# First attention of a two-layer kernel: probabilities normalised in the 16-bit cast, one PSUM bank for each head's queries

## The reference, cut to what matters

```
q, k, v = einsum('bsx,xAnh->Abnsh', input, qkv * c1)      # 16 heads of 64
q = q + q_bias
a = einsum('bnqh,bnkh->bnqk', q, k) * 64 ** -0.5
a = a + relative_causal(einsum('bnqh,nvh->bnqv', q, emb) * 64 ** -0.5)
a = softmax(where(tril, a, -1e9))                          # 512 x 512, causal
o = einsum('bnqk,bnkh->bqnh', a, v).reshape(b, s, 1024)
out = o @ (out_kernel * c2) + out_bias
x = layernorm(x + out)
```

## Time and profile before

| | |
|---|---|
| median of 3 runs | 1677.52 us (1674.55 to 1745.03) |
| the profiled execution | 1676.82 us |
| its span in the profile | 1675.1 us |
| granted TensorE clock, mean | 0.948 of 2.4 GHz |
| busiest engines over the span | PE 85%, DVE 75%, ACT 58%, POOL 53% |

### The profile page before, as it was taken

How to read it: one execution, slowest core, us unless ns; L and a number is a source line. 1 busy time by engine, 2 the same in 40 slices (tenths; PEclk the granted TensorE clock), 3 DMA queues, 4 the chain that set the end, 5 groups by cost and what they waited for, 6 DMA issues and landing times. The chain is left out here.

```text
span 1675.1 us, 38178 instructions
## 1 busy us (share of the span) xinstructions
PE 1421.9 (85%) x12519; PEld 834.2 (50%) x12519; DVE 1262.4 (75%) x2722; ACT 971.0 (58%) x1921; POOL 879.9 (53%) x1203
## 2 busy tenths in 40 slices
PE   4899989898998999897589887489899899898736
PEld 3566666666666666665356555123333333332216
DVE  3788888887888888886688888377787787777534
ACT  2677767676776767675244443156666666665431
POOL 2877778777787777775445555211221221222524
PEclk9899999999999999999699999599999999999977
DMA  5645545454454545544000000411011011010001
GB/s 160 123 113 127 123 98 125 97 122 110 110 125 105 114 111 118 116 110 94 0 2 0 0 0 0 146 48 35 27 39 36 26 39 36 26 40 28 13 12 27
DMA packets 372881, 116.47 MB, mean 70 GB/s; under 512 B 341675, under 2 KB 369312, under 8 KB 372704
## 3 DMA queue, kind: packets, MB, share of 16 engines
q1 hardware_dynamic: 369472, 111.36, 27.9%
q10 hardware_dynamic: 1824, 3.15, 0.6%
q0 software_dynamic: 1536, 1.34, 0.3%
HBM read 20.36 MB, written 12.89 MB: 20 GB/s over the span
## 5 line engine op out<-in xcount | busy, mean ns | idle before, releaser
L541 ACT ACTIVATE prob<-score_ps,nmax 128x512 f32<-128x512 f32 (+3 forms) x512 | 264.9, 526 | 209.0 <-DVE nmax L594 209.0
L1563 DVE TENSOR_REDUCE a_nm<-a_s 128x1 f16<-128x512 f32 x512 | 324.8, 687 | 55.5 <-PE a_s L1335 53.6
L1489 ACT ACTIVATE a_pt<-a_st 128x1024 f32<-128x1024 f32 x256 | 260.4, 1021 | 131.4 <-PE a_st L1353 116.3
L130 POOL TENSOR_TENSOR gate<-mhalf 128x1 f32<-128x1 f32 (+1 forms) x284 | 124.2, 437 | 259.3 <-ACT k L566 137.6
L1335 PE MATMUL a_s<-a_kop,a_qop 128*128 128x512 f16 x512 | 199.6, 391 | 64.2 <-DVE a_nm L1563 47.4
L606 DVE SCALAR_TENSOR_TENSOR p<-prob,p 128x1280 f16<-128x1280 f32 x128 | 204.6, 1598 | 49.8 <-ACT p L550 49.8
L594 DVE TENSOR_REDUCE nmax<-score_ps 128x1 f32<-128x512 f32 (+3 forms) x512 | 213.0, 475 | 3.4 <-PE score_ps L455 3.3
L452 PE MATMUL score_ps<-k_h,q_h 128*128 128x512 f16 (+3 forms) x512 | 158.2, 309 | 22.4 <-ACT prob L541 14.2
L550 ACT ACTIVATE p<-prob 128x1280 f16<-128x1280 f32 x128 | 163.8, 1279 | 6.5
L888 ACT ACTIVATE hid<-fps,b_cols 128x512 f32<-128x512 f32 x130 | 86.3, 687 | 127.2 <-PE fps L848 127.2
L694 POOL TENSOR_TENSOR q_l<-q,q_h 128x512 f16<-128x512 f32 x130 | 152.9, 1176 | 10.8
(11 more groups left out here) (331 smaller groups left out, 3433.5 us busy)
## 6 DMA issues: line engine op xcount, KB each, us to landing
a_qop<-q_parts SPq DMA_DIRECT2D x32, 128.0 KB
a_kop<-k_parts SPq DMA_DIRECT2D x128, 24.0 KB
x_tok<-in_L_attn_input_dram SPq DMA_DIRECT2D x4, 512.0 KB, 12.3
pt<-p SPq DMA_TRANSPOSE x128, 4.1
e_w<-in_L_ffn_w_dram SPq DMA_DIRECT2D x1, 2048.0 KB, 8.3
q_parts<-a_q_h SPq DMA_DIRECT2D x16, 128.0 KB
k_parts<-a_k_h SPq DMA_DIRECT2D x16, 128.0 KB
out_dram<-a_res SPq DMA_DIRECT2D x8, 256.0 KB
```

Of the source, the lines that this page charges most:

```text
L541: ins = nc.scalar.activation(prob[h][:, P_OFF[c]:P_OFF[c] + w], score_ps[u][:, col:col + w], ACT.Exp, bias=nmax[h][:, c:c + 1], accum_out= ...
L1489: nc.scalar.activation(pt[kc % 2][r][:, :, :], st_ps[r][:, :, :], ACT.Exp, scale=1.0 / SC).then_inc(exp_done[r], 1)
L1563: nc.vector.tensor_reduce(nm[g % 2][:, c, hh:hh + 1], s_ps[c % 2][:, :], AX.X, ALU.max, negate=True).then_inc(max_done[c % 2], 1)
```

## The change

The reciprocals, times the scale of the cast (now 64, not 1024), go straight into the cast. A row of `prob` has a reciprocal of its own for each of the four row blocks, so `high` on ACT becomes four instructions (128, 256, 384, 512 columns), each with a column of `rsum` as its scale, and `low` on DVE four scalar_tensor_tensors likewise. `reciprocals` gets a second instruction on the 4 columns, the product with the scale, behind a wait for the first. `high` waits for `r_done` of its head. The 16 matmuls into `r_ps`, `r_copy` and `normalise` go; in their place ACT copies `pv_ps` to `o32` (`o_copy`). The bank of `r_ps` becomes a second query bank: each head has its own `q_ps`, and `project_q` waits for the evacuation of its own head from the pair before. The order on DVE becomes: maxima 0, low 1 of the pair before, reciprocals 0, query evacuation 0, maxima 1, low 0, query evacuation 1, reciprocals 1, `v_low`. On ACT the key copy now follows all three banks of exponentials 0.

```
--- before.py
+++ after.py
@@ -33,7 +33,7 @@
...
 QK_SCALE = HD ** -0.25
-P_SCALE = 1024.0
+P_SCALE = 64.0
...
 E0, F0 = 8, 2 * D
@@ -300,18 +300,18 @@
...
         pt = [[sb(f"pt{h}{k}", [P, 2 * BLOCKS, P], F16) for k in range(2)] for h in range(2)]
-        r_sb = sb("r_sb", [P, S], F32)
         o32 = sb("o32", [P, S], F32)
...
         sums = [sb(f"sums{h}", [P, QC], F32) for h in range(2)]
-        rsum = [sb(f"rsum{k}", [P, QC, 2], F32) for k in range(2)]
+        rsum = [sb(f"rsum{h}", [P, QC], F32) for h in range(2)]
         y = sb("ln_y", [P, QC, D], F32)
...
         score_ps = [ps(f"score_ps{u}") for u in range(3)]
-        q_ps, kv_ps, pv_ps, r_ps, out_ps = ps("q_ps"), ps("kv_ps"), ps("pv_ps"), ps("r_ps"), ps("out_ps")
+        q_ps, pv_ps, out_ps = [ps(f"q_ps{h}") for h in range(2)], ps("pv_ps"), ps("out_ps")
+        kv_ps = ps("kv_ps")
...
         count = lambda n, u: 3 * n + u + 1
@@ -321,7 +321,8 @@
...
         turned = [pair(f"turned{h}") for h in range(2)]
-        pv_mm, r_out, o_done, out_mm, y_done = sem("pv_mm"), sem("r_out"), sem("o_done"), sem("out_mm"), sem("y_done")
+        pv_mm, o_done, out_mm, y_done = sem("pv_mm"), sem("o_done"), sem("out_mm"), sem("y_done")
+        r_steps = sem("r_steps")
         pool_steps, turn_open = sem("ra_pool"), sem("turn_open")
@@ -424,7 +425,7 @@
...
             def project_q(h, bx, pw):
-                project(q_ps, 128 * h, bx, pw).then_inc(q_mm[h], 1)
+                project(q_ps[h], 128 * h, bx, pw).then_inc(q_mm[h], 1)
...
                 project(kv_ps, 256, bx, pw).then_inc(k_mm, 1)
@@ -458,13 +459,8 @@
...
-                pe.wait_ge(r_done[1], n + 1)
                 if later(n, 1):
                     pe.wait_ge(o_done, n)
-                for c in range(QC):
-                    for h in range(2):
-                        nc.tensor.matmul(r_ps[64 * h:64 * h + 64, c * P:(c + 1) * P], rsum[k][:, c, h:h + 1].to_broadcast([P, 64]),
-                                         m.ident[:, :], start=True, stop=True)
                 pe.wait_ge(v_lo, n + 1)
...
                     pe.wait_ge(turned[h][k], 16 * (t + 1))
@@ -496,7 +492,6 @@
...
                 project_q(0, 0, 0)
-                pe.wait_ge(q_out[0], 1)
                 project_q(1, 0, 0)
...
             def body(n, t, b, p, k):
@@ -507,12 +502,12 @@
...
                 project_k(bx, pw)
-                pe.wait_ge(q_out[1], n + 1)
+                pe.wait_ge(q_out[0], n + 1)
                 project_q(0, bx, pw)
...
                 scores(1, n)
-                pe.wait_ge(q_out[0], n + 2)
+                pe.wait_ge(q_out[1], n + 1)
                 project_q(1, bx, pw)
...
                 project_v(b, p)
@@ -544,14 +539,19 @@
...
-                act.wait_ge(exp_done[h], count(n, 2))
+                act.wait_ge(r_done[h], n + 1)
                 if later(n, 2):
                     act.wait_ge(turned[h][k], 16 * t)
-                nc.scalar.activation(p16[h][k][:, 0, :], prob[h][:, :], ACT.Copy, scale=P_SCALE).then_inc(p_hi[h], 1)
-
-            def r_copy(n):
+                for c in range(QC):
+                    cs = slice(P_OFF[c], P_OFF[c] + P * (c + 1))
+                    ins = nc.scalar.activation(p16[h][k][:, 0, cs], prob[h][:, cs], ACT.Copy, scale=rsum[h][:, c:c + 1])
+                ins.then_inc(p_hi[h], 1)
+
+            def o_copy(n):
                 act.wait_ge(pv_mm, n + 1)
-                nc.scalar.activation(r_sb[:, :], r_ps[:, :], ACT.Copy).then_inc(r_out, 1)
+                if later(n, 1):
+                    act.wait_ge(out_mm, n)
+                nc.scalar.activation(o32[:, :], pv_ps[:, :], ACT.Copy).then_inc(o_done, 1)
...
                 act.wait_ge(v_mm, n + 1)
@@ -566,21 +566,19 @@
...
             def body(n, t, b, p, k):
-                exps(0, n, [0, 1])
+                exps(0, n, [0, 1, 2])
                 k_copy(n + 1)
-                exps(0, n, [2])
                 high(0, n, t, k)
                 if later(n, 2):
-                    r_copy(n - 2)
+                    o_copy(n - 2)
                 exps(1, n, [0, 1, 2])
...
                 n = B * PAIRS
-                r_copy(n - 2)
-                act.wait_ge(o_done, n - 1)
-                r_copy(n - 1)
+                o_copy(n - 2)
+                o_copy(n - 1)
...
             schedule(act, lambda: k_copy(0), body, last)
@@ -595,28 +593,26 @@
...
-            def reciprocals(h, n, k):
+            def reciprocals(h, n):
                 dve.wait_ge(exp_done[h], count(n, 2))
-                if later(n, 2):
-                    dve.wait_ge(pv_mm, n - 1)
-                nc.vector.reciprocal(rsum[k][:, :, h], sums[h][:, :]).then_inc(r_done[h], 1)
+                nc.vector.reciprocal(rsum[h][:, :], sums[h][:, :]).then_inc(r_steps, 1)
+                dve.wait_ge(r_steps, 2 * n + h + 1)
+                nc.vector.tensor_scalar(rsum[h][:, :], rsum[h][:, :], P_SCALE, None, ALU.mult).then_inc(r_done[h], 1)
...
                 dve.wait_ge(p_hi[h], n + 1)
-                nc.vector.scalar_tensor_tensor(p16[h][k][:, 1, :], prob[h][:, :], P_SCALE, p16[h][k][:, 0, :],
-                                               ALU.mult, ALU.subtract).then_inc(p_lo[h], 1)
+                dve.wait_ge(r_done[h], n + 1)
+                for c in range(QC):
+                    cs = slice(P_OFF[c], P_OFF[c] + P * (c + 1))
+                    ins = nc.vector.scalar_tensor_tensor(p16[h][k][:, 1, cs], prob[h][:, cs], rsum[h][:, c:c + 1], p16[h][k][:, 0, cs],
+                                                         ALU.mult, ALU.subtract)
+                ins.then_inc(p_lo[h], 1)
...
                 dve.wait_ge(q_split[h], n)
-                nc.vector.scalar_tensor_tensor(q32[h][:, :], q_ps[:, :], m_flat(m.q_bias)[:, ds(PAIRS * h + pw, 1)],
+                nc.vector.scalar_tensor_tensor(q32[h][:, :], q_ps[h][:, :], m_flat(m.q_bias)[:, ds(PAIRS * h + pw, 1)],
                                                m.q_mult[:, h, :], ALU.add, ALU.mult).then_inc(q_out[h], 1)
-
-            def normalise(n):
-                dve.wait_ge(r_out, n + 1)
-                if later(n, 1):
-                    dve.wait_ge(out_mm, n)
-                nc.vector.tensor_tensor(o32[:, :], pv_ps[:, :], r_sb[:, :], ALU.mult).then_inc(o_done, 1)
...
                 dve.wait_ge(v_hi, n + 1)
@@ -650,17 +646,15 @@
...
                 if later(n, 1):
-                    reciprocals(1, n - 1, 1 - k)
                     low(1, n - 1, 1 - k)
+                reciprocals(0, n)
                 q_evac(0, n + 1, pw)
...
                     batch_stats(b - 1)
+                maxima(1, n)
                 low(0, n, k)
-                if later(n, 2):
-                    normalise(n - 2)
-                reciprocals(0, n, k)
-                maxima(1, n)
                 q_evac(1, n + 1, pw)
+                reciprocals(1, n)
                 v_low(n, k)
...
                     add_bias(b)
@@ -674,10 +668,7 @@
...
                 n = B * PAIRS
-                reciprocals(1, n - 1, 1)
                 low(1, n - 1, 1)
-                normalise(n - 2)
-                normalise(n - 1)
                 batch_sum(B - 1)
...
                 batch_norm(B - 1)
```

30 lines of the change are left out of this document (10 added, 20 removed).

## The result

The changed kernel takes **1718.0 us** (median of 4 runs, 1716.6 to 1719.0), the kernel before, run beside it, 1676.2. The ratio is **1.025 [1.023, 1.027]**: slower, by 42 us; forecast were 1727 in a range of 1650 to 1785. One of the four runs of the kernel before was a slow one (1745 us), and the ratio leaves it out.

What follows compares the result with a forecast made beforehand. The prediction took a DVE-ACT relay, with DVE's lows and POOL's splits excluding each other on a nearly full SBUF path, as the bound. (11.8 - 11.02) x 64 = +50 us on 1676.8 gave 1727 us, range 1650 to 1785.

Steps and rivals of the forecast that it cites:

- The path: SBUF path shared by POOL's splits and DVE's lows: 8.6 + 2 x 1.85 = 12.3, less 0.5 overlap, 11.8 us.
- the sum over DVE: DVE's side of a pair: 9.5 us without waits, plus 1.9 in a low and 0.6 for products, 12.0.
- The low's pieces: DVE's low in four instructions: 0.343, 0.475, 0.61, 0.74 us; 1.85 against 1.38 together, +0.47, twice a pair.
- ACT's cast: ACT's high cast in four instructions: 1.7 us against about 1.2, 0.5 more, twice a pair; ACT stays under the period.
- A: The forecast case, slower: DVE and POOL exclude each other on a full shared path; 1727 us, chance 0.60.
- rival D: Within A, on ACT: late high 0 delays exponentials 1; ACT's 10.1 us stays under 11.8; no separate chance.
- PE: PE stands beside the relay: removing 16 spreading matmuls (0.92 us a pair) and adding the second query bank count 0.
- DVE's idle times: DVE's two idle times before a low and before the values' low part, 2.02 us a pair, can go by the new order.
- The sum: Whole stage: (11.8 - 11.02) x 64 = +50 us on 1676.8, giving 1727; layer norms at batch ends left as they are.

Runs made afterwards that it cites:

- the short subtractions: Changed kernel with POOL subtracting only 128 of 512 columns in each of the four splits a pair, leaving out part of the computation; ratio to the kernel before 0.968.
- the keys off POOL: Changed kernel without the product (scale 1), keys' split moved to ACT casts and DVE subtractions from PSUM, keys double buffered; ratio to the kernel before 0.998.

## Why the prediction was right, and where it was off

**The path** (11.8 a pair): the pair measured 11.83, and the mechanism held: DVE's idle time went and waits inside its instructions came. Two experiments that touch no work of DVE in the pairs (the short subtractions) or one instruction of it (the low in four, before) turn the waits off and on. The forecast split of the waits was off: low 0 lets in 1.26, not 1.9; one product waits 0.93 and the other nothing, where I had 0.2 to 0.4 for each. Together that is 2.19, where the sum over DVE had 2.5. DVE's own work came to 11.83 - 2.19 = 9.64, forecast 9.5. The reason that I gave for picking 11.8 over 12.0, that the path is full, is not the law: with POOL pausing three times a pair, lows still waited 0.9 each. And the path was not full here, for POOL idles 2.55 us in the pair, 0.6 more than the low of 1.92 beside it takes. The direction came from the mechanism; that 11.8 was hit to 0.03 is luck.

**The low's pieces** were right: 0.345, 0.477, 0.611 and 0.744 us where nothing waits, against 0.343, 0.475, 0.61 and 0.74; the four end to end 1.92 at their best.

**ACT's cast** was slightly under-sized: from the start of the four pieces to the start of what follows it is 1.82 (387.93 to 389.75), forecast 1.7. The rows are 402, 493, 600 and 707 ns for 128 to 512 columns. The formula for a pointer bias in "ScalarE: Activation LUTs", section "What ACT_TABLE_LOAD costs", in the Trainium skill (280 ns and 0.833 ns a column) gives 387, 493, 600 and 707; here the pointer is the scale, and the rows agree within 15 ns. I called the cast harmless inside A (rival D, "it matters only in B"); putting it back whole gave 2.0%, so that step failed. POOL's idle before its first key split grew to 2.55, where I expected under 1.53: POOL starts by ACT's key copy, and that now comes later. With the cast whole the idle was 1.94, so 0.6 of the growth is the longer cast; the rest may be the key copy's new place behind the third bank, which no run tests.

**PE**: the matmuls (14 of 16 left out in the kernel before, all 16 put back in the changed one) and the bank were forecast at 0 and measured 0, with the offset told above for the matmuls in the changed kernel.

**DVE's idle times** went as forecast, but I gave the new order the credit alone. By itself it costs 2.5% (1.025).

**The sum**: 0.81 x 64 = 52 us for the steady pairs, forecast 50. The term that was mis-sized is that of the batch ends, "which I leave as they are": what a batch takes beside its eight pairs fell from 92.86 - 8 x 11.02 = 4.7 to 98.25 - 8 x 11.83 = 3.6, eight times 1.1. With that, 52 - 9 = 43, where 42 were measured. Why a batch's end got shorter I have not followed.

**The parts do not add.** Taking away the product, making the low whole or making the cast whole give 2.6, 3.0 and 2.0%, together 7.6%, where the whole change cost 2.5%. That need not be a contradiction, since each also takes work away, the first two from DVE (0.5 and 0.9 us a pair) and the third from ACT, and the change had 2.02 us of idle time to win. Each also moves the moment at which POOL's instructions meet DVE's. Open are why without the product short and long pairs take turns, and by what rule the path is given out between two instructions; the runs show only that a waiting POOL instruction gets in.

## What to carry to other kernels

Where VectorE and GpSimd share a path, look at what becomes ready on GpSimd while VectorE is between two instructions that need it. In this kernel the one instruction with two SBUF inputs let nothing in, and cut in four, with the same columns, it cost 2.4%: 0.2 us a pair of own work and 0.5 of waiting. Look for such waits in the scatter of the durations of one and the same instruction, not in idle time or busy shares: both engines look busy while they wait. And read the waits before the page: the engine with the highest share, PE at 85%, gave nothing back for 14 matmuls fewer a pair. Last, an experiment that removes an instruction removes its work and its waits together. The runs that decided here left VectorE's work alone (the short subtractions) or moved work onto it (the keys off POOL).

## What the runs showed of the hardware

- A tensor_scalar on four fp32 columns from SBUF to SBUF took 0.17 us or up to 1.10, by what GpSimd was doing; the reciprocal of as many columns beside it took 0.16 to 0.18 in each of its 128 records. "SBUF — State Buffer", section "SBUF: two separate sides", in the Trainium skill speaks of a lock held for the whole instruction; the product that ends 0.03 us behind a subtraction agrees.
- A scalar_tensor_tensor with two SBUF inputs, fp32 to fp16, that 128 to 512 columns kept busy for 345 to 744 ns with half of GpSimd's work gone took 408 to 1096 ns on average beside GpSimd's four splits a pair.
- The waiting stands in the records of both engines: GpSimd's subtraction of 1.16 us took 2.27 where it started 0.31 us behind a VectorE instruction of 1,280 columns.
